# Self-attention with a plasticity scan in three stages instead of five, in a decoder on one core of Trainium2

## The reference

```python
qkv = (x @ Wqkv_w + Wqkv_b).reshape(Bb, Ll, 3, Hh, dd)
scores = jnp.einsum('bhid,bhjd->bhij', q, k) * scale
attn = jax.nn.softmax(scores + causal_mask, axis=-1)
y_softmax = jnp.einsum('bhij,bhjd->bhid', attn, v)
retention = 1.0 - jax.nn.sigmoid(Lambda_raw)
def step(state, inp):
    q_t, k_t, v_t = inp
    hebbian = v_t[..., :, None] * k_t[..., None, :]
    state = retention * state + Gamma * hebbian
    y_t = jnp.einsum('bhij,bhj->bhi', W_static + state, q_t)
    return (state, y_t)
g = jax.nn.gelu(x @ gate_w1 + gate_b1, approximate=False)
alpha = jax.nn.sigmoid(g @ gate_w2 + gate_b2)
y = alpha * y_softmax + (1.0 - alpha) * y_stp
return y @ out_w + out_b
```

## Time and profile before

| | us |
|---|---|
| median of 3 runs | 7213.0 (7208.46 to 7213.35) |
| profiled execution | 7213.07 |
| its span | 7211.4 |
| projections q, k and v | 40.7 to 168.3 |
| attention stage | 168.3 to 608.0 |
| mixing stage | 608.0 to 980.4 |

### The profile page before, as it was taken

The page is one execution under the profiler, slowest core; times in us unless marked ns, Lnnn a source line. Parts: engine busy times, 40 slices in busy tenths (PEclk is TensorE's granted clock), DMA queues, the critical chain, the costliest instruction groups (busy, mean ns, idle before and its releaser), DMA issues. The chain is left out here.

```text
span 7211.4 us, 140243 instructions
## 1 busy us (share of the span) xinstructions
PE 5480.0 (76%) x46501; PEld 2956.1 (41%) x46547; DVE 4981.5 (69%) x9029; ACT 3299.7 (46%) x4728; POOL 2005.8 (28%) x2590
## 2 busy tenths in 40 slices
PE   3686657688888848960686999997666699999759
PEld 1343335222222223420454888886534233333334
DVE  5564663799999943447897777773553599999654
ACT  0233424477676722230684444443223477777512
POOL 1101324577676720000004555551303200000000
PEclk6898978799999968985897888886777799999979
DMA  2220016222222200000233344332205322222200
GB/s 60 49 45 9 7 31 202 83 60 56 57 60 55 56 30 19 0 2 0 98 127 120 114 118 113 114 113 65 67 15 174 117 66 63 65 64 63 61 11 12
DMA packets 756737, 475.96 MB, mean 66 GB/s; under 512 B 517528, under 2 KB 683264, under 8 KB 754880
## 3 DMA queue, kind: packets, MB, share of 16 engines
q1 hardware_dynamic: 756416, 471.66, 23.2%
HBM read 273.95 MB, written 196.37 MB: 65 GB/s over the span
## 5 line engine op out<-in xcount | busy, mean ns | idle before, releaser
L1481 ACT ACTIVATE c0a_raised<-c0a_sb 128x1024 f32<-128x1024 f32 (+1 forms) x832 | 837.1, 1026 | 318.0 <-PE c0a_sb L1293 314.9
L1246 POOL TENSOR_SCALAR c0a_prob<-c0a_raised 128x1024 f32<-128x1024 f32 (+1 forms) x832 | 866.0, 1041 | 382.4 <-ACT c0a_raised L1481 351.8
L1481 ACT ACTIVATE c1a_prob<-c1a_sb 128x1024 f32<-128x1024 f32 (+1 forms) x832 | 828.9, 1029 | 205.4 <-PE c1a_sb L1293 201.9
L1369 DVE TENSOR_REDUCE c0a_pmax<-c0a_sa 128x2 f32<-128x802 f32 (+1 forms) x704 | 696.9, 990 | 76.0 <-PE c0a_sa L1261 71.9
L1369 DVE TENSOR_REDUCE c1a_pmax<-c1a_sa 128x2 f32<-128x802 f32 (+1 forms) x704 | 698.1, 992 | 70.7 <-PE c1a_sa L1261 66.7
L1261 PE MATMUL c0a_sa<-c0a_K,c0a_Q 48*128 48x401 bf16 (+1 forms) x2048 | 475.5, 351 | 191.7 <-DVE c0a_pmax L1369 104.7
L1261 PE MATMUL c1a_sa<-c1a_K,c1a_Q 48*128 48x401 bf16 (+1 forms) x2048 | 466.1, 346 | 103.6 <-DVE c1a_pmax L1369 46.0
L1312 PE MATMUL c0a_pv<-c0a_prob,c0a_V 128*9 128x256 f32 x6656 | 529.6, 390 | 4.8 <-POOL c0a_prob L1246 4.1
L1312 PE MATMUL c1a_pv<-c1a_prob,c1a_V 128*9 128x256 f32 x6656 | 519.4, 383 | 0.7 <-issue 0.5
L1261 PEld LDWEIGHTS c0a_sa<-c0a_K,c0a_Q 48*128 48x128 bf16 x2048 | 130.0, 94 | 680.3 <-DVE c0a_pmax L1369 331.7
L2924 PE MATMUL dd_lb<-dd_src 64*128 64x128 f32 (+1 forms) x3584 | 359.3, 347 | 39.0 <-POOL dd_src L2907 15.9
(11 more groups left out here) (594 smaller groups left out, 11592.0 us busy)
## 6 DMA issues: line engine op xcount, KB each, us to landing
unit_in<-dp_res SPq DMA_DIRECT2D x64, 512.0 KB, 2.6
dd_src<-unit_in SPq DMA_DIRECT2D x64, 512.0 KB, 6.4
k_ctx<-c0k_parts SPq DMA_DIRECT2D x16, 1200.8 KB, 4.7
c0a_K<-k_ctx SPq DMA_DIRECT2D x128, 150.1 KB
k_ctx<-c1k_parts SPq DMA_DIRECT2D x16, 1200.8 KB, 4.7
c1a_K<-k_ctx SPq DMA_DIRECT2D x128, 150.1 KB
unit_v<-dp_vs SPq DMA_DIRECT2D x64, 256.0 KB, 2.8
dd_l_img<-dd_AB SPq DMA_DIRECT2D x64, 256.0 KB
```

Of the source, the lines that this page charges most:

```text
L1246: pool.tensor_scalar(prob[0:r, in_ring(v, c), :, :, :], raised[0:r, in_ring(v, c), :, :, :], 1.0, math.exp(-FLOOR), ALU.min, ALU.max).then ...
L1369: dve.tensor_reduce(pmax[:, u, :, 2 * pr + s, k], sa2[:, :, 0:w], AX.X, ALU.max).then_inc(a_reduced, 1)
L1481: act.activation(dst[0:r, in_ring(v, c), :, :, :], sb_[0:r, in_both(v, c), :, :, :], ACT.Exp).then_inc(b_exp, 1)
```

## The change

Five stages become three. In the instruction lists below, those headed "Now" have the line numbers of the changed kernel.

- `self_project` (names q_) takes the place of both `project_stage` calls, of `value_stage`, and of the projections in `mix_stage`. It works on 512 columns at a time: q, k and v, the gate's hidden layer, v by rows with a one behind each head's eight values, the three-way splits (q's on VectorE, k's differences on GpSimd), and alpha for all positions. Its queue issues 8 weight and 64 parameter transfers, then eight stores for each chunk.
- `self_attention` (names s_) runs the attention in 64 units of four heads, written out without a loop, in the form of the cross-attention: K and Q in two halves of 49 rows (the 49th, from krow and qrow, masks the block above the diagonal) plus three rows of maxima. Into each unit it lays two of the scan's 128 rows. ScalarE scales k by Gamma, GpSimd multiplies by v (each channel of v is broadcast from DRAM over its head), VectorE scans, ScalarE adds W_static, GpSimd multiplies by q, TensorE sums. The output goes to y_rows undivided, with its sum.
- `self_out` (names m_) is `cross_out` with the mixing: each batch is scaled, mixed with the scan's result and alpha in four products, 11 batches on VectorE and 5 on GpSimd, projected and added.

```diff
-def value_stage(nc, name, XT, w, bias, dst):
-def attention_stage(nc, name, q_parts, k_parts, v_units, y_units, ident, keys, groups, causal=False, clip=False):
-def mix_stage(nc, name, X, XT, ident, t, y_units):
+def self_project(nc, name, XT, t, q_parts, k_parts, q_full, k_full, v_full, v_rows, alpha, gamma, retain, static, select):
+            def _(sp):
...
+                for c in range(CHUNKS):
+                    u = c % 2
+                    sp.wait_ge(v_ready, c + 1)
+                    sp.dma_start(by_batch(v_full, c), halves(fv[:, u, :])).then_inc(v_stored[u], 16)
+                    sp.wait_ge(rows_ready, c + 1)
+                    sp.dma_start(v_rows[2 * c:2 * c + 2].rearrange("a p k x -> p a (k x)"),
+                                 vt[:, u, :, :, :].rearrange("p (a k) h d -> p a (k h d)", a=2)
+                                 ).then_inc(rows_stored[u], 16)
+                    sp.wait_ge(q_step, 5 * c + 5)
+                    sp.dma_start(by_batch(q_full, c), halves(fq[:, u, :])).then_inc(q_stored[u], 16)
+                    for a in range(2):
+                        sp.dma_start(q_parts[2 * c + a].rearrange("c p t -> p c t"),
+                                     parts_q[:, u, :, a * L:(a + 1) * L]).then_inc(q_stored[u], 16)
...
+                for c in range(CHUNKS):
+                    pe.wait_ge(g_ready, c + 1)
+                    if c >= 1:
+                        pe.wait_ge(a_ready, c)
+                    pe.matmul(ap[:, :], gw2e[:, :], gT[:, c * C:(c + 1) * C], start=True, stop=True
+                              ).then_inc(a_projected, 1)
...
+def self_attention(nc, name, q_parts, k_parts, v_rows, y_rows, q_full, k_full, v_full, stp, gamma, retain, static, select,
+                   ident):
...
+                def load(n):
+                    v, b, x = n % LOADS, n // 4, n % 4
+                    kd = k_parts[b].rearrange("c (d x e r) t -> e x (c d) r t", d=HD, x=4, e=2)[:, x]
+                    qd = q_parts[b].rearrange("c (d x e r) t -> e x c d r t", d=HD, x=4, e=2)[:, x]
+                    if n >= LOADS:
+                        sp.wait_ge(b_scored, (n - LOADS + 1) * KT)
+                    r = 0
+                    for (first, count), (cq, _count) in zip(K_LOADS, Q_LOADS):
+                        for e in range(2):
+                            at = slice(e * HALF + r * HD, e * HALF + (r + count) * HD)
+                            sp.dma_start(K[at, v, :, :], kd[e, first * HD:(first + count) * HD]
+                                         ).then_inc(K_loaded[v], 16)
+                            sp.dma_start(Q[at, v, :, :], qd[e, cq:cq + 1].to_broadcast([count, HD, 2, L])
+                                         ).then_inc(K_loaded[v], 16)
+                        r += count
...
+                sp.wait_ge(set_up, 7)
+                for v in range(LOADS):
+                    for e in range(2):
+                        at = slice(e * HALF + ROWS, e * HALF + MASKED)
+                        sp.dma_start(K[at, v, :, :], krow[:, :, :]).then_inc(rows_set, 16)
+                        sp.dma_start(Q[at, v, :, :], qrow[:, :, :]).then_inc(rows_set, 16)
+                for n in range(2):
+                    load(n)
+                load_plastic(0)
+                for n in range(2, LOADS - 1):
+                    load(n)
+                load_plastic(1)
+                for n in UNIT_RANGE:
+                    if 0 <= n and n + LOADS - 1 < UNITS:
+                        load(n + LOADS - 1)
+                    if 4 <= n < UNITS - 4 and n % 4 == 1:
+                        load_plastic(n // 4 + 1)
+                    if 0 <= n + 2 < UNITS:
+                        put_maxima(n + 2)
+                    if 0 <= n < UNITS:
+                        put_y(n)
...
+def self_out(nc, name, X, ident, y_rows, y_scale, stp, alpha, wo, bo):
+    ON_POOL = [b for b in range(B) if b % 3 == 1]
...
+            eng.tensor_tensor(mixed[:, b, :], y[:, b, :], r[:, b, :], ALU.mult).then_inc(step, 1)
+            eng.wait_ge(step, 3 * k + 1)
+            eng.tensor_tensor(mixed[:, b, :], mixed[:, b, :], stp[:, b, :], ALU.subtract).then_inc(step, 1)
+            eng.wait_ge(step, 3 * k + 2)
+            eng.tensor_tensor(mixed[:, b, :], mixed[:, b, :], alpha_v[:, b, :], ALU.mult).then_inc(step, 1)
+            eng.wait_ge(step, 3 * k + 3)
+            eng.tensor_tensor(mixed[:, b, :], mixed[:, b, :], stp[:, b, :], ALU.add).then_inc(done, 1)
...
             norm_stage(nc, "n0", X, XT, ident)
-            project_stage(nc, "q0", XT, w, bias, HD ** -0.5, q_parts, 0)
-            project_stage(nc, "k0", XT, w, bias, 1.0, k_self, P)
-            value_stage(nc, "v0", XT, w, bias, v_self)
-            attention_stage(nc, "s0", q_parts, k_self, v_self, y_units, ident, L, H // HG, causal=True)
-            mix_stage(nc, "m0", X, XT, ident, t, y_units)
```

More of the change, by code:

```diff
@@ L1688, in _ @@
-                over_pairs(sp, B, unit)
-            LOADS = 16 * (10 + 5 * H)
+                w, b = t["L0_attn_Wqkv_w"], t["L0_attn_Wqkv_b"]
+                with nc.allow_non_contiguous_dma(reason="one parameter for each partition"):
+                    for dst, src in [(w_in[:, :, :], w.rearrange("p (c x) -> p c x", c=3)),
+                                     (bq[:, :], by_dimension(b, 0)), (bk_in[:, :], by_dimension(b, P)),
+                                     (bvc[:, :], column(b, 2 * P)), (bv[:, :], b[2 * P:3 * P].partition_broadcast(P)),
+                                     (gw1[:, :], t["L0_attn_gate_w1"]),
+                                     (gb1[:, :], column(t["L0_attn_gate_b1"], 0, D // 2)),
+                                     (gw2[:, :], t["L0_attn_gate_w2"])]:
+                        sp.dma_start(dst, src).then_inc(loaded, 16)
+                    for h in range(H):
+                        rows = slice(h * HD, (h + 1) * HD)
+                        for dst, src in ((gamma, t["L0_attn_Gamma"]), (lam, t["L0_attn_Lambda_raw"]),
+                                         (static, t["L0_attn_W_static"])):
+                            sp.dma_start(dst[rows, :], src[h].rearrange("i j -> j i")).then_inc(params_loaded, 16)
+                        sp.dma_start(gb2[rows, :], t["L0_attn_gate_b2"][h:h + 1].partition_broadcast(HD)
+                                     ).then_inc(params_loaded, 16)
@@ L1759, in plasticity_sum, with ready_of @@
[L1759 to L1765 removed]
+                pe.wait_ge(w_sorted, 4)
+                def ready_of(j):
+                    return (q_ready, k_ready, v_ready)[j % 3], j // 3 + 1
@@ L1798, in _ @@
+                act.wait_ge(params_loaded, PARAMS)
+                act.activation(retain[:, :], lam[:, :], ACT.Sigmoid, scale=-1.0)
+                for c in range(CHUNKS):
+                    act.wait_ge(a_projected, c + 1)
+                    act.activation(alpha[:, c * C:(c + 1) * C], ap[:, :], ACT.Sigmoid, bias=gb2[:, 0:1]
+                                   ).then_inc(a_ready, 1)
             @block.vector
```

1193 lines of the change are left out of this document (559 added, 634 removed).

## The result

The median of the changed kernel is 7139.2 us (7132.36 to 7149.64, four runs), that of before 7213.2 us: ratio 0.990, interval 0.9882 to 0.9917. The profiled execution took 7144.65 us, its span is 7142.8 us. Forecast were 7108 us and 7040 to 7190.

What follows compares the result with a forecast made beforehand. In the old attention TensorE was busy 341 of 440 us, in mixing no engine was near full; SyncE's queue would bound the new attention. Next norm at 875 instead of 980.5: 7213.07 - 105 = 7108 us, range 7040 to 7190.

Steps and rivals of the forecast that it cites:

- The mechanism: In the new attention SyncE's queue of transfer issues is the longest engine and sets a period of 9.7 us a unit.
- projections, to the next stage: Projection stage: stores, then alpha products ending at 146 us; GpSimd starts the next stage at 147.
- memsets and one-row transfers: Attention's start: about 6 us waiting for memsets, then 24 one-row transfers at 0.35 us (8.4).
- first five loads to the loop's first: Attention's start: five loads (34.1 us), six scan transfers (3.8) and two pairs of maxima (3.2), to 202.5 us.
- 59 loads: Attention's steady state: 59 units carrying a load at 9.7 us each, 572.3 us, to 774.8.
- units without loads, drain: Attention's end: five units without loads at 6.3 us (31.5), then 12 us for scan drain and last store, to 818.
- output stage to the norm: Output stage: 55 us with VectorE's products and additions on the path, the norm 2.3 us later, 57 in all.
- The step that had the stores of a chunk: Projection stage: each of eight chunks stores 1.87 MB at 212 GB/s, 8.8 us a chunk, 70.5 us, to 137.7.
- The first two pairs of maxima: Attention's start: two pairs of maxima at 1.61 us each, 3.2 us, before masked scores can start.
- TensorE did not become the bound: Rival for the attention, 8%: TensorE falls to 1.2 GHz and becomes the bound, 7279 us.
- The rings: Rival for the attention, 8%: rings back up, each unit's start costs 1.2 us more, period 10.9, 7179 us.
- The queue hides: Rival for the attention, 12%: issue is cheaper or loads drop out, VectorE sets about 6.3 us a unit, 6907 us.

Runs made afterwards that it cites:

- wide_loads: Changed kernel with K and Q of a batch's four units loaded in one set of 12 wider transfers, one-row transfers cut from 24 to 4: 6933.5 us (0.9608).
- spread_only: Wide K and Q loads and the scan's broadcast spread over a batch's units, maxima and output first, parameter transfers ahead of the first store: 6854.5 us (0.9501).
- maxima_first: Changed kernel with each unit's maxima and output ahead of the loads in SyncE's attention queue, same number of transfers: 7131.3 us (0.9885).
- code_plus100: Changed kernel with 100 more TensorE instructions (satisfied waits) ahead of the first cross-attention's loop: 7157.0 us (0.9927).
- code_both: Changed kernel with 200 satisfied waits ahead of TensorE's first cross-attention loop and 312 ahead of the second: 7087.8 us (0.9822).
- spread: Wide K and Q loads and the scan's broadcast spread over a batch's units, maxima and output first, parameter transfers behind the projection stores: 6864.9 us (0.9522).
- wide_code: Changed kernel with wider K and Q loads, plus waits that put TensorE's two cross-attention loops at the addresses of the 7087.8 us run: 6956.8 us (0.9644).
- code_plus1: Changed kernel with 1 more satisfied wait ahead of TensorE's loop in the first cross-attention: 7126.3 us (0.9881).
- no_scan_loads: Changed kernel without the scan's input transfers of batches 2 to 15, its arithmetic kept: 7088.0 us (0.9835).
- params_late: Changed kernel with the projection stage's 64 parameter transfers moved behind the stores of the first six chunks: 7142.1 us (0.9905).
- code_plus50: Changed kernel with 50 more TensorE instructions (satisfied waits) ahead of the first cross-attention's loop: 7149.0 us (0.9920).
- before_code_plus100: Kernel of before the change with 100 more TensorE instructions ahead of the first cross-attention's loop: 7286.2 us (1.0096).

## Why the prediction was right, and where it was off

**The mechanism was right.** SyncE issues at 9.0 us a unit and 9.8 on average (59 loads from 202.28 to 780.2, 577.9 us; forecast 572.3), with waits for maxima of 21.5 us in all that time; no engine is near full, and the waits of s_sb name s_mrows. Taking the issue away took the time away (wide_loads, spread_only); taking only the order away did not (maxima_first). By the Trainium skill's section on issuing engines (DMA: Bandwidth & Descriptors) the queue would have been hidden; here the measurement decides against it, 9.0 us of issue for 16 transfers.

**The terms**, forecast and measured:

| | forecast | measured | |
|---|---|---|---|
| projections, to the next stage | 147 | 131.3 | -15.7 |
| memsets and one-row transfers | 14.4 | 21.7 | +7.3 |
| first five loads to the loop's first | 41.1 | 49.3 | +8.2 |
| 59 loads | 572.3 | 577.9 | +5.6 |
| units without loads, drain | 43.2 | 32.9 | -10.3 |
| output stage to the norm | 57 | 54.3 | -2.7 |
| next norm | 875 | 867.4 | -7.6 |
| from there to the end | 6230.9 | 6275.4 | +44.5 |

That the next norm came within 8 us of the forecast is in part luck: three terms were 29 us too high together, three 21 us too low. The total, 31 us above the forecast, stayed in the range, although the 44.5 us behind the change were in none of the terms that the range was made of.

*Projections.* The step that had the stores of a chunk, 1.87 MB at 212 GB/s, set 8.8 us was mis-sized: a chunk took 5.7 to 6.2 us. From 81.04 to 110.57 us the DMA engines moved 312 GB/s and were busy 0.96 of the time, and VectorE 28.5 of 29.5 us, so both limits lay at 6 us and which of them set it was not tested. The row of the context stage from which the rate came has an average with gaps in it, not a limit. The alpha products took 2.91 us each, a little over the bound of 2.7.

*One-row transfers* took 0.63 us each, not 0.35. The nearest row had been that of transfers from DRAM; these come from SBUF. That this is the reason was not tested.

*The first two pairs of maxima* took 9.6 us behind the scan's broadcast (192.67 to 202.24), not 3.2. The prediction had named this cost at every fourth unit (0.35 a unit; measured 21.5 us of waits in 59 units, 0.36), and not at the start.

*K, Q, maxima and scan inputs* were read from rows of the same shapes and held within 2%: 6.29 for 6.36, 1.58 for 1.61, 0.64 for 0.64. V took 0.63 for 0.46: the price had come from another shape, while the cross-attention's V, 0.60, stood in the earlier trace rows. The units without loads, put at 6.3, came 7.7, 5.3 and 4.7 us apart (maxima at 781.44, 789.11, 794.37 and 799.07).

**The step that failed** was unspoken: that the work behind the change keeps its time. The sum took the next norm's start, 980.5, against the new one and let all the rest stand. 33 of the 44.5 us are the stops in the first cross-attention; by the runs the stage takes 1199 to 1202 us from first to last reduction without stops (code_plus100, code_both, wide_loads, spread_only), 1217 with 3, and 1249 to 1265 with 13 (1250 in the changed kernel). The other 11 us are not shown to have a cause: from the norm ahead of the first experts to the one ahead of the second cross-attention, a stretch that no edit touches, the runs take between 2744 and 2755 us (2744.4 before, 2754.4 after, 2743.9 in wide_loads, 2754.6 in spread).

**The rivals.** TensorE did not become the bound, though its clock was lower than forecast (0.75): it stands idle 1.5 to 3.4 us for the maxima in three units of four and 8.1 to 10.3 us in the fourth, and behind such a long pause the products take 0.61 instead of 0.39. The rings did not back up: no transfer of K or Q in the stage took over 0.85 us to issue. *The queue hides* has its number in spread_only, 6.2 us a unit where the rival had 6.3, but not its reason: there TensorE is the longest engine, and VectorE is busy 149 of 200 us, not over 80%.

**Where a loop stays loaded.** In straight code there is one packet for each 256 instructions (26 in the changed attention stage, some 6540 instructions without a loop). So the packets' starts, set against TensorE's own instructions on the first pass through a stage, tell how far behind the start of such a block the loop begins. That is an estimate, good to some 10 instructions; it gives back the known edits of 50, 100 and -48 instructions within that. The first and the second cross-attention of all fourteen kernels, in this order of places:

| loop begins behind a block's start by | kernels | stops at 13 jumps back |
|---|---|---|
| 1 to 24 | first: code_plus100, code_both, wide_code; second: before, wide_loads, spread, spread_only | 0 |
| 55 to 68 | second: after, code_plus1, code_both, wide_code, maxima_first, no_scan_loads, params_late | 0 |
| 105 to 113 | first: wide_loads, spread, spread_only; second: code_plus50 | 0 |
| 110 | first: before | 3 |
| 122 | second: before_code_plus100 | 4 |
| 159 to 201 | first: after, code_plus1, code_plus50, before_code_plus100, maxima_first, no_scan_loads, params_late; second: code_plus100 | 13 |

Seven blocks hold 1792 instructions, 121 more than the loop's 1671. So a loop that fits into seven blocks stayed loaded, one that reaches into an eighth was fetched anew at every jump back, and at the edge both happen within one execution: the two loops there lie closer together than the estimate can tell apart from those without stops. The change took the first loop from that edge into the eighth block. This rule was read from the traces when all runs were done; none was made to test it, and what decides from turn to turn at the edge stays open. The Trainium skill (Runtime: NRT & Kernel Launch, Instruction fetch mechanics) says that code comes in blocks of 16 KiB and that a taken branch whose target is outside a window of two pages must wait for a fetch. Block size and stop agree; that every back jump of a loop this long would stop does not, since a loop of seven blocks had no stop.

## What to carry to other kernels

Count the transfers of a stage and multiply by the issue time of the same shape from a stage that already runs: where the product is the longest engine, make the transfers wider before anything else, then spread them so that no small urgent transfer stands behind a large one. After any change to a long program compare the time of the stages that were not changed, and read the code queue's packets: a loop of over a thousand instructions on one engine can gain or lose 50 us by where it stands, and a comparison of two kernels carries that along. Its place is better read from when the packets start than from a count made by hand. A rate read from a stage's average is no bound for another.

## What the runs showed of the hardware that was not expected

- TensorE's loop of 1671 instructions stayed loaded where it fitted into seven blocks of 256. Where it reached into an eighth: 9 packets of 16 KB and a stop of 2.9 to 3.6 us at each jump back, and with the lower clock behind it some 3.9 us a time in the first cross-attention and 5.5 in the second.
- 100 instructions that only wait for what is already there made a kernel 73 us slower, or moved 50 us of stops from one stage to another.
- A transfer of 8 to 24 rows with 4 KB each took SyncE mostly 0.57 to 0.80 us to issue (wide_loads, medians 0.66 for K and 0.69 for Q), one with 1 KB each 0.26 to 0.85 (medians 0.42 and 0.66): four times the bytes for at most 1.6 times the issue.
- A transfer of one row of 1 KB from SBUF to SBUF took 0.59 us to issue, and 0.63 with its gap.
